# Second stage of a banded linear plus FP8 linear block: where y, b2 and gelu live, who makes the low parts, and four buffers of transposed parts

## The reference

```python
xn   = layernorm(x)
attn = einsum('ds,td->st', w1, w2) * sparse_mask          # 1024 x 1024, a band around the diagonal
y    = gelu(einsum('bds,st->bdt', xn, attn) + b2)         # exact gelu
w_q  = (weight * w_scale) in float8_e4m3,  x_q = (xn * x_scale) in float8_e5m2   # scales from the largest |value|
ffn  = einsum('bsk,nk->bsn', x_q, w_q) / x_scale / w_scale + bias
out  = x + y + ffn
```

## Time and profile before

| | us |
|---|---|
| median of 3 runs (lowest, highest) | 296.73 (296.45, 297.36) |
| the profiled execution | 297.18 |
| its span, first to last instruction | 295.4 |
| outside the span | 1.78 |

### The profile page before, as it was taken

One profiled execution on the slowest core, in us unless ns is written; L12 is line 12 of the kernel. 1 busy time (PEld: TensorE's weight loads), 2 busy tenths in 40 slices (PEclk: granted clock), 3 DMA queues, 4 the chain that ended last, 5 costly groups with the idle time before them and its releaser, 6 DMA issues.

```text
span 295.4 us, 4915 instructions
## 1 busy us (share of the span) xinstructions
PE 251.4 (85%) x1818; PEld 174.7 (59%) x1818; DVE 224.5 (76%) x222; ACT 204.7 (69%) x239; POOL 246.5 (83%) x140
## 2 busy tenths in 40 slices
PE   0049799990299899999999999999999989999992
PEld 0038688870297476667666666666666557666650
DVE  3888989999977389997758966574994666666544
ACT  1089989999975798596666948667576568775210
POOL 2000699999995799999999999999999999999991
PEclk9999999997559999999999999999999999999998
DMA  6999999999974449999999999999999879998923
GB/s 248 416 410 409 409 408 409 407 385 409 307 188 93 77 81 217 196 232 223 222 209 223 257 201 241 215 211 270 201 210 177 232 100 235 218 179 231 228 93 145
DMA packets 99721, 72.56 MB, mean 246 GB/s; under 512 B 85488, under 2 KB 87280, under 8 KB 99696
## 3 DMA queue, kind: packets, MB, share of 16 engines
q1 hardware_dynamic: 99696, 72.24, 90.2%
HBM read 34.60 MB, written 16.78 MB: 174 GB/s over the span
## 4 chain that ended last, share of the span: by engine, by line
POOL 51%; DMA 15%; ACT 9%; issue 8%; DVE 7%; SPq 5%; PE 3%; POOLq 1%; ACTq 0%; DVEq 0%
POOL x_all L538 23%; POOL x_all L532 19%; DMA home<-home 8%; DMA x_all<-in_L_attn_w_dram 4%; SPq L364 3%; POOL wq_nat L472 3%; POOL x_all L468 3%; DMA x_all<-in_L_attn_x_dram 3%; PE psT L981 2%; POOL rs L481 2%; ACT xq L679 2%; ACT squares L576 2%; ACT junk L563 2%; DVE x_all L907 2%; DVE maxsq L777 2%
## 5 line engine op out<-in xcount | busy, mean ns | idle before, releaser
L538 POOL TENSOR_TENSOR x_all<-x_all,home 128x1024 f32<-128x1024 f32 x31 | 88.2, 2844 | 3.8 <-ACT home L691 0.2
L532 POOL TENSOR_TENSOR x_all<-x_all,biases 128x1024 f32<-128x1024 f32 x32 | 83.5, 2610 | 0.6 <-ACT wq_nat L686 0.6
L894 DVE TENSOR_TENSOR home<-home 128x1024 f16<-128x1024 f32 x28 | 55.5, 1983 | 9.3 <-ACT home L672 9.3
L1065 PE MATMUL psT<-wqT,wq_nat 128*128 128x512 f16 x256 | 57.9, 379 | 1.6 <-ACT wq_nat L686 1.3
L1065 PE MATMUL psF<-wqT,wq_nat 128*128 128x512 f16 x256 | 57.9, 379 | 0.0
L691 ACT ACTIVATE home<-home 128x1024 f32<-128x1024 f32 x32 | 33.6, 1051 | 27.3 <-DVE home L901 27.3
L672 ACT ACTIVATE home<-home 128x1024 f16<-128x1024 f32 x28 | 29.6, 1057 | 31.1 <-DMA home<-home 30.8
L1048 PE MATMUL psZ<-split,home 128*128 128x197 f16 (+2 forms) x480 | 44.2, 249 | 0.9 <-DMA home<-home 0.9
L1048 PE MATMUL psY<-split,home 128*128 128x197 f16 (+2 forms) x480 | 44.2, 249 | 0.2 <-DMA home<-home 0.2
L1048 PEld LDWEIGHTS psZ<-split,home 128*128 128x128 f16 x480 | 38.3, 97 | 8.3 <-DMA home<-home 1.7
L1048 PEld LDWEIGHTS psY<-split,home 128*128 128x128 f16 x480 | 38.3, 97 | 7.6 <-DMA home<-home 1.0
(11 more groups left out here) (96 smaller groups left out, 293.7 us busy)
## 6 DMA issues: line engine op xcount, KB each, us to landing
x_all<-in_L_attn_x_dram SPq DMA_DIRECT2D x32, 512.0 KB, 14.0
out_dram<-x_all SPq DMA_DIRECT2D x31, 512.0 KB, 3.3
x_all<-in_L_attn_w_dram SPq DMA_DIRECT2D x16, 512.0 KB, 15.3
x_all<-in_L_ffn_weight_dram SPq DMA_DIRECT2D x8, 512.0 KB, 7.6
squares<-_L_attn_sparse_mask_dram SPq DMA_DIRECT2D x2, 413.5 KB, 4.0
biases<-_L_attn_sparse_mask_dram SPq DMA_DIRECT2D x6, 133.0 KB, 11.0
squares<-_L_attn_sparse_mask_dram SPq DMA_DIRECT2D x2, 349.5 KB, 3.3
squares<-_L_attn_sparse_mask_dram SPq DMA_DIRECT2D x2, 285.5 KB, 3.3
```

The source lines that it names most:

```text
L532: nc.gpsimd.tensor_tensor(x_all[:, SLOT[q], :], x_all[:, SLOT[q], :], bias_bc, ALU.add)\
L538: nc.gpsimd.tensor_tensor(x_all[:, SLOT[q], :], x_all[:, SLOT[q], :], t1[:, q % 2, :], ALU.add).then_inc(u_ready, 1)
L894: nc.vector.tensor_tensor(hl[:, q % 2, D:2 * D], xs[:, q % 2, :], hl[:, q % 2, 0:D], ALU.subtract).then_inc(xl_ready, 1)
L1065: ins = nc.tensor.matmul(ps_f[q % 2][:, HALF * h:HALF * h + HALF], quantised(q % XQ_RING)[:, k // 2, k % 2, :], wqT[:, k, HALF * h:HALF * ...
```

## The change

- The `t1` buffers are gone. `add_b2` writes its result back into `psY` or `psZ`, where it read it, and ScalarE's gelu works there in place.
- VectorE adds gelu from PSUM to the tile in `x_all` (a new `add_gelu`). It signals `u_ready`. GpSimd's `add_bias` now comes after it (waits for `u_ready`), and `finish` waits for `bias_added` in place of `u_ready`. Before, the order at the tile was bias, gelu, FP8 product; now it is gelu, bias, FP8 product.
- `attn(q + 2)` waits for `u_ready` of tile q in place of `t1_ready`: the PSUM is held until gelu has been added.
- GpSimd makes all low parts (`low` moves from VectorE), after `add_bias(q)` the one of tile q + 4.
- The two slots of `t1` go to `hlT`, which gets four buffers; `transpose_parts(q)` waits for `y_done` of tile q - 4.
- The extra code for gelu of tile 31 on VectorE goes.

```diff
@@ shapes and buffers
-WQ_RING, SQ_RING, XQ_RING = 4, 3, 4
+WQ_RING, SQ_RING, XQ_RING, HLT_RING = 4, 3, 4, 4
...
-        hlT = home[:, 4:6, :].bitcast(F16)
-        t1 = home[:, 6:8, :]
+        hlT = home[:, 4:8, :].bitcast(F16)
...
-        def wait_low(eng, q):
-
-            eng.wait_ge(first_low if q < FIRST else xl_ready, q + 1 if q < FIRST else q - FIRST + 1)
+        def wait_hlT(eng, q):
+
+            eng.wait_ge(hlT_loaded[q % HLT_RING], 16 * (q // HLT_RING + 1))
@@ SP
             def transpose_parts(q):
-                wait_low(sp, q)
-                if q >= 2:
-                    sp.wait_ge(y_done, q - 1)
-                sp.dma_start(hlT[:, q % 2, :].rearrange("p (k r) -> p k r", r=P), hl[:, q % 2, :],
-                             transpose=True).then_inc(hlT_loaded[q % 2], 16)
+                sp.wait_ge(xl_ready, q + 1)
+                if q >= HLT_RING:
+                    sp.wait_ge(y_done, q - HLT_RING + 1)
+                sp.dma_start(hlT[:, q % HLT_RING, :].rearrange("p (k r) -> p k r", r=P), hl[:, q % 2, :],
+                             transpose=True).then_inc(hlT_loaded[q % HLT_RING], 16)
@@ GpSimd
+            def low(q):
+                wait_xs(pool, q)
+                nc.gpsimd.tensor_tensor(hl[:, q % 2, D:2 * D], xs[:, q % 2, :], hl[:, q % 2, 0:D],
+                                        ALU.subtract).then_inc(xl_ready, 1)
...
             def add_bias(q):
                 pool.wait_ge(biases_loaded, 32)
-                wait_xs(pool, q)
-                pool.wait_ge(xq_ready, q + 1)
+                pool.wait_ge(u_ready, q + 1)
...
-            def add_gelu(q):
-                pool.wait_ge(gelu_ready, q + 1)
-                pool.wait_ge(bias_added, q + 1)
-                nc.gpsimd.tensor_tensor(x_all[:, SLOT[q], :], x_all[:, SLOT[q], :], t1[:, q % 2, :],
-                                        ALU.add).then_inc(u_ready, 1)
-
-            add_bias(0)
-            add_gelu(0)
-            add_bias(1)
             for q in range(NT):
-                if q + 1 < NT - 1:
-                    add_gelu(q + 1)
-                if q + 2 < NT:
-                    add_bias(q + 2)
+                add_bias(q)
+                if q + AHEAD < NT:
+                    pool.wait_ge(xh_ready, q + AHEAD - FIRST + 1)
+                    low(q + AHEAD)
@@ ScalarE
             def high(q):
                 wait_xs(act, q)
-                act.wait_ge(hlT_loaded[q % 2], 16 * (q // 2))
+                wait_hlT(act, q - 2)
...
             def gelu(q):
                 act.wait_ge(t1_ready, q + 1)
-                act.activation(t1[:, q % 2, :], t1[:, q % 2, :], ACT.Gelu).then_inc(gelu_ready, 1)
+                act.activation(ps_y[q % 2][:, :], ps_y[q % 2][:, :], ACT.Gelu).then_inc(gelu_ready, 1)
@@ VectorE
-            def low(q):
-                dve.wait_ge(xh_ready, q - FIRST + 1)
-                nc.vector.tensor_tensor(hl[:, q % 2, D:2 * D], xs[:, q % 2, :], hl[:, q % 2, 0:D],
-                                        ALU.subtract).then_inc(xl_ready, 1)
-
             def add_b2(q):
                 dve.wait_ge(y_done, q + 1)
-                if q >= 2:
-                    dve.wait_ge(u_ready, q - 1)
-                nc.vector.scalar_tensor_tensor(out=t1[:, q % 2, :], in0=ps_y[q % 2][:, :], scalar=y_mul,
-                                               in1=b2_bc, op0=ALU.mult, op1=ALU.add).then_inc(t1_ready, 1)
+                y = ps_y[q % 2][:, :]
+                nc.vector.scalar_tensor_tensor(out=y, in0=y, scalar=y_mul, in1=b2_bc, op0=ALU.mult,
+                                               op1=ALU.add).then_inc(t1_ready, 1)
+
+            def add_gelu(q):
+                x_q = x_all[:, SLOT[q], :]
+                dve.wait_ge(gelu_ready, q + 1)
+                wait_xs(dve, q)
+                dve.wait_ge(xq_ready, q + 1)
+                nc.vector.tensor_tensor(x_q, ps_y[q % 2][:, :], x_q, ALU.add).then_inc(u_ready, 1)
 
             def finish(q, cols=slice(0, D)):
-                dve.wait_ge(u_ready, q + 1)
+                dve.wait_ge(bias_added, q + 1)
...
+            add_gelu(0)
             for q in range(NT):
                 if q + 1 < NT:
                     add_b2(q + 1)
-                if q + AHEAD < NT:
-                    low(q + AHEAD)
                 if q >= 3 and q % 2 == 1 and q // 2 - 1 < KB:
                     count_mask(q // 2 - 1)
+                if q + 1 < NT:
+                    add_gelu(q + 1)
...
@@ TensorE
             def attn(q):
-                pe.wait_ge(hlT_loaded[q % 2], 16 * (q // 2 + 1))
+                wait_hlT(pe, q)
                 if q >= 2:
-                    pe.wait_ge(t1_ready, q - 1)
+                    pe.wait_ge(u_ready, q - 1)
```

23 lines of the change are left out of this document (8 added, 15 removed).

## The result

The changed kernel takes **293.62 us** in the median of 4 runs (291.98 to 293.77), the kernel before 296.59 in 4 runs (296.30 to 297.36). The ratio is **0.9896**, 95% interval 0.9861 to 0.9931: about 1% faster, and the interval does not reach 1. The profiled execution took 293.77 us (before 297.18), its span 292.0 us (before 295.4).

What follows compares the result with a forecast made beforehand. TensorE was taken to bound the second stage, running without a gap but for 1.96 us. From the profiled 297.18, -1.96 + 0.3 - 1.6 + 0.15 = -3.1 gave 294.1, in medians 293.6 us, range 292.6 to 295.6.

Steps and rivals of the forecast that it cites:

- The gaps: TensorE's second stage: all four gaps, 1.96 us in sum, would go, with 0.3 us held back.
- The end: After the last ffn: VectorE and GpSimd would finish the last tile 1.6 us sooner (1.3 to 1.7).
- The first round: Ahead of attn(2): TensorE would wait for VectorE's first gelu addition, costing 0.15 us (0 to 0.4).
- A loop that keeps pace with TensorE, not one that holds it: Second stage: GpSimd's 5.45 us a round stays under TensorE's 6.055, so a faster GpSimd wins at most 1.96 us of gaps.
- `low` off VectorE, four buffers: VectorE and transposes: without low, and with earlier transposes allowed, the queue would start with 1 to 3 us more in hand.
- Transposes 8 to 13 us ahead: DMA queue: parts would be transposed 8 to 13 us before their attn; tile 9's was 7.2 before.
- rival A: DMA queue, 0.99 busy: no lead builds up, gaps stay and only the end is won; 295.3 us, chance 0.18.
- The 0.3 kept back in the sum: TensorE's second stage: 0.3 us reserved in the sum for a gap that stays.
- The single prices: Operations: low on GpSimd 2.13 us, add_bias 2.36, add_gelu 1.25, PSUM writes at old durations; POOL's share some 75%.
- VectorE's round: Second stage: VectorE's work plus standing still for gelu makes 5.15 us a round, 0.9 under TensorE's 6.055.
- rival C: VectorE's round: PSUM writes cost half again, round 6.3 us, TensorE follows; 301.7 us, chance 0.11 with kindred ways.
- Rival B: Mask rounds: VectorE's waits in count_mask for late masks exceed 5.6 us and eat the gain; 296.7 us, chance 0.07.

Runs made afterwards that it cites:

- b0: The kernel before, unchanged, profiled once more: 295.97 us, ratio to itself 1.0001.
- b2: The kernel before, with VectorE instead of GpSimd adding gelu for tile 30 as well as 31, from SBUF: 296.06 us, ratio 0.9995.
- b3: The kernel before, with only tiles 30 and 31 done the change's way (gelu in PSUM, added by VectorE): 294.33 us, ratio 0.9958.
- a0: The changed kernel, unchanged, run once more: 293.67 us, ratio 0.9906 to the kernel before.
- b4: The kernel before, with GpSimd's deviations and scales of tiles 12 to 31 computed once in round 2, not in five batches: 293.33 us, ratio 0.9918.
- e4: The changed kernel with the low parts of tiles 4 to 31 back on VectorE: 293.27 us, ratio 0.9916 to the kernel before.
- e1: The changed kernel with two buffers of transposed parts instead of four: 293.04 us, ratio 0.988 to the kernel before.
- e2: The changed kernel with two buffers of transposed parts, and add_b2's result and gelu in SBUF: 294.90 us, ratio 0.9964 to the kernel before.
- e3: The changed kernel with mask loads and counts in every third round instead of every second: 292.50 us, ratio 0.9863 to the kernel before.
- e7: The changed kernel plus two dead VectorE operations of 1024 columns in each round: 326.14 us, ratio 1.102 to the kernel before.
- e5: The changed kernel plus one dead VectorE operation of 400 columns in each round: 294.12 us, ratio 0.994 to the kernel before.
- e6: The changed kernel plus one dead VectorE operation of 1024 columns in each round: 294.94 us, ratio 0.9996 to the kernel before.

## Why the prediction was right, and where it wasn't

- **The total.** 293.6 was forecast and 293.62 measured. Against its own profiled run the sum said -3.1 and the profile says -3.4. That the medians agree to 0.02 us is luck, since the parts of the sum repeat to half a us only.
- **The gaps.** -1.96 + 0.3 was forecast, -1.58 came; `ffn(30)` at 280.74 (280.6 to 281.2 was said). The size holds between these two profiles. In others the kernel before has 1.56, 1.42 and 0.64 (b0, and the first 30 rounds of b2 and b3), the changed one 0.54. The agreement is in part luck.
- **The end.** -1.6 was forecast, -1.68 came (1.04 between b0 and a0, since the end of before varies too). The last `finish` ends 4.40 us after the last `ffn` starts, 4.5 was said. As said, its first half waits for `add_bias` (to 287.02) and its second for the last product (284.30 + 3.62 = 287.92). The steps of the end were worked out right.
- **The first round.** +0.15 was forecast, nothing came: `attn(2)` starts 3.45 us after `ffn(0)`, as undisturbed. Gelu took 1.01 us from 99.59 and `add_gelu(0)` ran from 100.69 to 101.92, ahead of the first weights at 102.03. These weights start 3.32 us after `ffn(0)`, before 3.24: the wait was there, 0.08 us long, and the products behind them did not start later for it.
- **"A loop that keeps pace with TensorE, not one that holds it": wrong.** This is the step that failed, and it didn't change the sum. The prediction counted 5.45 us a round for GpSimd and put the deviations on top in words, but never compared four rounds of both: 24.9 us of work, 25.7 from start to start, against 24.22. TensorE's timeline shows few gaps because the buffers let GpSimd fall 7.3 us behind before TensorE waits (`ffn(22)`, 0.31 us); the end then pays. b4 shows that for the end: with 9.3 of the 15.5 us of GpSimd's small operations taken away it has the changed kernel's length, and its median gain (2.4 us) is no smaller than that of a0 (2.1). The sum was right, because the most that a faster GpSimd can win is what TensorE's timeline leaves, whatever the cause.
- **`low` off VectorE, four buffers.** The prediction credited both with a part. e4 (low parts on VectorE, no gap, 293.27) and e1 (two buffers, 293.04) show that neither is needed. What wins in the change is that GpSimd loses the addition of gelu, and that VectorE takes it from PSUM (e2: from SBUF 1.9 us of it are lost).
- **Transposes 8 to 13 us ahead: wrong where it would matter.** The queue in the changed kernel:

```profile
136.90 3.30 SPq L371 DMA_TRANSPOSE home<-home  x1
...
204.65 4.48 SPq L371 DMA_TRANSPOSE home<-home  x1
```

Tile 9's is issued 7.6 us before its `attn` (144.53), against 7.2 before, and from there to tile 20 it is 6.16 us a tile. Only behind the masks does the lead grow, to 11.8 us for tile 31. ScalarE waits more for the landing, not less (40.2 us in 26 waits, before 30.8 in 21). The low part of tile 9 is ready 11.6 us ahead of its `attn` in both kernels, and its transpose is issued 4.0 us after that (before 4.3), when the queue comes to it. What is gone are the low parts that were ready only 6 us ahead, as tile 25's. A queue that can't build up a lead under its load is rival A's mechanism. It is seen here, and small: 0.28 and 0.12 us, nothing in e3. The 0.3 kept back in the sum was the right size for it.
- **The single prices.** `low` on GpSimd 2.13 (2133 measured), `add_bias` 2.36 (2361), `add_gelu` 1.25 (1225), all at the value taken. PSUM writes at the old durations: +13 ns on `add_b2`, -48 ns on gelu. The Trainium skill's statement (ScalarE: Activation LUTs, "Step-by-step: what each stage is for") that ScalarE writes PSUM faster than SBUF fits the latter, but gelu now also reads PSUM, and no run here separates the two. POOL's share fell to 70%, not 75%.
- **VectorE's round: mis-sized.** 5.15 us with 0.9 to spare was forecast, it is 4.7 with 1.36: its operations were summed at their listed durations, and 1.35 us were put down for gelu and the hand-overs, where VectorE stands still for 1.07. Past that point TensorE pays the excess in every round, as rival C had it (e7); the point itself was put too near.
- **Rival B** did not come: VectorE's waits for masks are 4.4 us in 5 in the whole stage, 1.3 at most, and 5.6 were to spare.

**What stays open.** `ffn(0)` starts anywhere from 97.56 to 99.17 us over these profiles, without a pattern that follows the edits; that is as much as half the gain. The two kernels that were profiled twice repeated theirs to 0.01 and 0.22 us, while b3, b4, e1, e2, e3 and e5 all start between 97.56 and 97.80; whether the start belongs to an execution or to a kernel, and so how much of the medians of b3 and b4 it makes, isn't known. e5 had 1.81 us of gaps, in the mask rounds and with the DMA as releaser, where e6 with twice the extra work had 0.71; what the smaller operation does there wasn't found. How much of the gaps that the change wins is due to GpSimd's lag isn't known either: it was traced for the gaps at 233 and 243 alone.

## What to carry to other kernels

Compare two engines over the whole period after which their work repeats (here four rounds, with the deviations), and over the whole stage, not over the common round: an engine that needs 24.9 us where the other needs 24.2 falls behind, though 5.45 stands against 6.05, and the end shows it (190.3 us of the stage against 188.8). When an engine is full to 97%, look first for the small operations on it: taking out 9 us of them shortened the end as much as the restructuring did. What such an edit can win at most is read from the bounding engine's timeline (its gaps and its end), and that holds even where the reason for them is misread; gaps under 1 us want more than one profile.

## What the runs showed of the hardware

- Operations that follow each other on VectorE start sooner than their listed durations say: 1.23 us is followed 1.14 later, 1.28 us 1.19 to 1.20 later. Over a round of e6, with four of them, that is a quarter of a us. A hand-over between VectorE and ScalarE takes 0.03 us (282.23 to 282.26, and 283.27 to 283.30), less than the 0.11 from GpSimd to VectorE (287.02 to 287.13).
- GpSimd's `pow` on 128x4 took 1.04 us in three of the five batches of the kernel before and 1.91 to 1.92 in two; on 128x20 it took 3.57 in b4. The batch of five operations costs 3.1 to 3.3 us for 4 columns and 6.2 for 20, so five times the columns for twice the time.
- TensorE's clock fell at the end of e7, after it had stood still for 3.31 us. The windows of e7, before and after:

```profile
300.00:312.00 12.00, 8.25 (x56) 4.51 (x53) 10.42 (x9) 1.48 (x2) 4.69 (x2) 1.00 0.21 69
312.00:318.00 6.00, 5.43 (x17) 2.10 (x17) 4.93 (x7) 1.01 (x1) 2.16 (x1) 0.72 0.21 87
```

The granted clock goes from 1.00 (2.4 GHz) to 0.72 in the mean, and the 16 products of `ffn(31)` take 5.17 us in place of 3.62: 1.55 of the 4.1 us by which its end is longer. The idle time of 0.69 us a round before that left the clock at 1.00.
